# A gated cross-attention block: the attention tile normalised once, and its query brought to both partition halves by two identity matmuls

## What is computed

```
x += tanh(gx[0]) * attention0(layernorm(x), ctx, ctx)      # 32 query heads of 8, 8 key heads; keys = values = ctx
x += tanh(gf[0]) * experts(layernorm(x))                    # 64 experts, top 8 of each row, and a shared one
x += tanh(gx[1]) * (attention1(layernorm(x), ctx, ctx) @ Wc.T + bc)   # 16 query heads of 16, 4 key heads
x += tanh(gf[1]) * fp8_mlp(layernorm(x))                    # 256 -> 1024 -> 256, relu squared, emulated fp8
```

## Time and profile before

| | |
|---|---|
| runs (3), device time | 1719.53 us median, 1709.69 to 1721.87 |
| profiled execution, span | 1714.7 us |
| granted clock of PE, mean over the span | 0.803 of full speed |
| first attention | up to about 296 us |
| experts | about 296 to 1168 us |
| second attention | about 1168 to 1520 us |
| mlp | the rest |

### The profile page before, as it was taken

How to read it: one execution, slowest core, us unless ns; L and a number is a source line. 1 busy time by engine, 2 the same in 40 slices (tenths; PEclk the granted TensorE clock), 3 DMA queues, 4 the chain that set the end, 5 groups by cost and what they waited for, 6 DMA issues and landing times.

```text
span 1714.7 us, 32329 instructions
## 1 busy us (share of the span) xinstructions
PE 1178.8 (69%) x9122; PEld 778.6 (45%) x9132; DVE 1084.7 (63%) x2699; ACT 783.1 (46%) x1599; POOL 883.5 (52%) x846
## 2 busy tenths in 40 slices
PE   4999998133333299999678777871676777846775
PEld 2566665112221266666555555650454444532243
DVE  5899996666666466666444454442765555747898
ACT  3566665122222166666445454441343333433574
POOL 2343343266666633333377777715888888516100
PEclk9999999555555599999777887785788888878878
DMA  9555554032323599999899999984344434100011
GB/s 209 161 151 154 148 154 135 15 115 104 111 106 110 154 281 308 310 301 304 206 242 237 252 246 248 247 199 101 53 54 55 55 55 55 28 1 1 13 37 49
DMA packets 283470, 247.09 MB, mean 144 GB/s; under 512 B 117584, under 2 KB 270032, under 8 KB 282960
## 3 DMA queue, kind: packets, MB, share of 16 engines
q1 hardware_dynamic: 234192, 169.99, 38.9%
q0 software_dynamic: 49152, 75.53, 20.8%
HBM read 111.93 MB, written 117.77 MB: 134 GB/s over the span
## 4 chain that ended last, share of the span: by engine, by line
DMA 24%; DVE 20%; PE 18%; POOL 16%; issue 13%; SPq 4%; ACT 3%; DVEq 1%; POOLq 0%; ACTq 0%
DMA xs<-V 13%; POOL x L632 11%; DMA arena<-xs 8%; PE bank L1493 4%; DVE arena L1318 3%; DMA xs<-arena,V 2%; PE bank L1369 2%; POOL rs L575 2%; PE bank L1381 2%; DVE arena L971 2%; PE bank L1355 2%; PE bank L1569 2%; PE bank L1370 2%; SPq L518 2%; DVE arena L1316 2%
## 5 line engine op out<-in xcount | busy, mean ns | idle before, releaser
L632 POOL DMA_INDIRECT x<-ys,idx x256 | 404.1, 1578 | 129.2 <-issue 57.6
L650 POOL DMA_INDIRECT xs<-V x192 | 187.1, 974 | 207.7 <-DMA xs<-V 188.5
L1493 PE MATMUL bank<-arena,region 128*128 128x128 f16 x2496 | 253.2, 245 | 1.6 <-ACT arena L834 0.9
L834 ACT COPY arena<-bank 128x640 f16<-128x640 f16 x192 | 132.3, 689 | 190.2 <-PE bank L1569 188.2
L1569 PE MATMUL bank<-arena 128*128 128x128 f16 x1440 | 145.2, 240 | 105.3 <-DMA arena<-xs 101.5
L1381 PE MATMUL bank<-arena 128*72 128x256 f32 (+1 forms) x768 | 212.0, 417 | 0.1
L1493 PEld LDWEIGHTS bank<-arena,region 128*128 (+1 forms) x2496 | 187.0, 111 | 19.2 <-issue 6.2
L1569 PEld LDWEIGHTS bank<-arena 128*128 128x128 f16 x1440 | 97.0, 107 | 113.3 <-DMA arena<-xs 85.4
L573 POOL TENSOR_TENSOR ve<-mv,epsilon 128x1 f32<-128x1 f32 x96 | 39.5, 412 | 202.0 <-DVE mv L912 180.0
L1381 PEld LDWEIGHTS bank<-arena 128*72 128x72 f32 (+1 forms) x768 | 117.2, 158 | 46.4 <-issue 13.5
L982 DVE TENSOR_REDUCE arena<-bank 128x8 f32<-128x512 f32 x192 | 124.1, 675 | 15.5 <-PE bank L1355 14.3
(11 more groups left out here) (204 smaller groups left out, 2557.6 us busy)
## 6 DMA issues: line engine op xcount, KB each, us to landing
ys<-arena SPq DMA_DIRECT2D x96, 512.0 KB
arena<-xs SPq DMA_DIRECT2D x288, 160.0 KB
xs<-idx SPq DMA_DIRECT2D x52, 256.0 KB, 2.4
arena<-in_wpairs SPq DMA_DIRECT2D x32, 256.0 KB, 2.6
arena<-in_wpairs SPq DMA_DIRECT2D x128, 64.0 KB, 2.5
x<-ys,idx POOLq DMA_INDIRECT x256, 6.3
out<-arena SPq DMA_DIRECT2D x16, 256.0 KB, 2.2
xs<-idx SPq DMA_DIRECT2D x52, 64.0 KB, 2.1
```

Source lines behind the costliest of these rows:

```text
L632: pool.indirect_dma_start(tile_x(t), None, ys[t // HT], bass.IndirectOffsetOnAxis(ap=idx[:, t, k:k + 1], axis=0), compute_op=ALU.add).then ...
L650: pool.indirect_dma_start(xs[t // HT], bass.IndirectOffsetOnAxis(ap=at_row[:, t, n % 8:n % 8 + 1], axis=0), ROW[t % NROW], None).then_inc( ...
L834: act.copy(XTP[g % 2][q], tpm[n % 2]).then_inc(R_["xt"], 1)
L1493: mm = pe.matmul(o, lhs(a, w, k), rhs(a, w, k), start=(n == 0), stop=(n == 3 * KT - 1))
```

## The change

`norm` writes one destination. XG loses its first copy: a group is now 64 columns and the maxima's. L1435 turns columns 0 to 71 in place of 64 to 135. Where L1422 was one transpose for a group, there are now two plain fp32 matmuls with the identity as the moving operand, the 64 columns of XG as weights, the first into PSUM partitions 0 to 63, the second into 64 to 127. The waits and the semaphores stay as they are.

```diff
--- before.py
+++ after.py
@@ -247,7 +247,7 @@
 
 
     W0 = C + 8
-    XG = [carve([G, C + W0]) for _ in range(2)]
+    XG = [carve([G, W0]) for _ in range(2)]
     KM = carve([2 * 8 * S], F16)
     Q1 = [carve([G, P], F16) for _ in range(2)]
     Q2 = [carve([G, P], F16) for _ in range(2)]
@@ -914,9 +914,7 @@
             def norm(t, j, layer, dst, src):
                 l = LNS[layer]
                 dve.wait_ge(l["rs"], STAT_BASE[layer] + t + 1)
-                for d in dst[:-1]:
-                    dve.tensor_scalar(d, src, mv[:, j, 0:1], rs[:, j, :], ALU.subtract, ALU.mult)
-                dve.tensor_scalar(dst[-1], src, mv[:, j, 0:1], rs[:, j, :], ALU.subtract, ALU.mult).then_inc(l["out"], 1)
+                dve.tensor_scalar(dst, src, mv[:, j, 0:1], rs[:, j, :], ALU.subtract, ALU.mult).then_inc(l["out"], 1)
 
             def biggest(dst, src, done):
                 dve.tensor_reduce(dst, src, AX.X, ALU.max, apply_absolute_value=True).then_inc(done, 1)
@@ -979,7 +977,7 @@
                 def maxima(t, j, u):
                     n = t * nmx + u + 1
                     dve.wait_ge(a["mx_ready"], n)
-                    dve.tensor_reduce(XG[j][:, u * gpu:(u + 1) * gpu, 2 * C:C + w],
+                    dve.tensor_reduce(XG[j][:, u * gpu:(u + 1) * gpu, C:w],
                                       bank[2 + u % 2][:, :].rearrange("p (g k t) -> p g k t", g=gpu, t=S),
                                       AX.X, ALU.max).then_inc(a["mx_done"], 1)
 
@@ -1031,12 +1029,11 @@
 
                         if past(t, 4):
                             dve.wait_ge(F["tp_ready"], t - 3)
-                        norm(t - 2, 2 + j, 3, [XD[j]], tile_x(t - 2))
+                        norm(t - 2, 2 + j, 3, XD[j], tile_x(t - 2))
                     if inside(t + 3):
                         if past(t, -1):
                             dve.wait_ge(a["t2_ready"], t + 2)
-                        norm(t + 3, 1 - j, ln, [XG[1 - j][:, :, r * C:(r + 1) * C].rearrange("p g (k d) -> p g k d", d=d) for r in range(2)],
-                             heads(tile_x(t + 3)))
+                        norm(t + 3, 1 - j, ln, XG[1 - j][:, :, 0:C].rearrange("p g (k d) -> p g k d", d=d), heads(tile_x(t + 3)))
                     if layer == 1 and inside(t - 2):
                         dve.wait_ge(LND["out"], t - 1)
                         dve.tensor_reduce(AM[:, bass.ds(t - 2, 1)], XD[j], AX.X, ALU.max, apply_absolute_value=True).then_inc(F["am_done"], 1)
@@ -1419,8 +1416,8 @@
                         if layer == 1 and past(t, 4):
                             pe.wait_ge(F["xf_ready"], t - 3)
                         for g in range(G):
-                            mm = pe.transpose(bank[0][:, g * P:(g + 1) * P],
-                                              XG[j][:, g, 0:2 * C], ident)
+                            for half in range(2):
+                                mm = pe.matmul(bank[0][half * C:(half + 1) * C, g * P:(g + 1) * P], XG[j][:, g, 0:C], ident, start=True, stop=True)
                         mm.then_inc(a["t1_ready"], 1)
                     if inside(t):
                         values(t, j, 0)
@@ -1432,7 +1429,7 @@
                         if layer == 1 and past(t, 2):
                             pe.wait_ge(a["x_done"], t - 1)
                         for g in range(G):
-                            mm = pe.transpose(bank[1][0:w, g * P:(g + 1) * P], XG[1 - j][:, g, C:C + w], ident)
+                            mm = pe.transpose(bank[1][0:w, g * P:(g + 1) * P], XG[1 - j][:, g, 0:w], ident)
                         mm.then_inc(a["t2_ready"], 1)
                     if inside(t - 1) and layer == 1:
                         pe.wait_ge(a["on_ready"], t)
```

## The result

The changed kernel takes 1718.4 us (median of 20 runs, 1713.6 to 1727.2) and the kernel before 1710.5 (20 runs taken beside them): a ratio of 1.0052, 95% interval 1.0034 to 1.0070. That is 0.5% slower, which is clear over 20 runs; the first three runs of the kernel before alone have a median of 1719.5, above the changed kernel's. One run of the kernel before took 2526.7 us and is left out of the comparison. The profiled execution has a span of 1719.8 us against 1714.7.

A forecast was written before the change was run, and what follows sets the result against it. DVE's loop was taken to bound the first attention and mostly POOL's gathers the second. Terms 6.3 + 2.4 − 0.7 = +8.0 us gave 1727.5 on the 1719.5 median, own range 1722 to 1733, 1715 to 1756 with rivals.

The forecast's parts named there:

- What bounds it: First attention: a loop through DVE sets 8.15 us a tile, PE alone 7.93; second attention: mostly POOL's gathers.
- DVE: One of two norm passes goes per tile and layer, saving 0.40 us, not 1.16; in the first attention it falls into DVE's pause.
- one use: First attention: the removed pass lets the first two L982 finish 0.22 us sooner when PE moves up against L1028.
- PE's term: Query transposes: eight fp32 matmuls take 0.97 us in place of 0.50, +0.47 a tile, range 0.36 to 1.22.
- the rival with long steps: Query matmuls take nine steps of 0.133 us, +0.70 a tile; +16 us in all, 1735 us; chance 0.14.
- the serial rival: fp32 records in different PSUM halves don't overlap, +1.22 us a tile; +33.5 in all, 1753 us; chance 0.23.
- Sum, first attention: Tile goes from 8.15 to 8.40 us: +6.3 over 25 tiles, +2.4 for five earlier ones, nil for the first two.
- they take all: First attention, 32 to 72 us: five early no-wait tiles each bear the full 0.47 us, +2.4 together.
- Second attention: PE's extra time hides under POOL; −1.1 for gathers, +1.2 in the last four tiles, −0.8 in the first two: −0.7 us.
- The −1.1 for POOL's gathers: Second attention: the first gather after a norm, 1.61 us with L919 beside it against 1.56 next, gains 28 x 0.04 us.
- The +1.2 of the four tiles at the end: Second attention's last four tiles: PE waits 0.32 us for L1028, so 0.15 of each +0.47 shows, the first two whole.
- the rival "no effect": TensorE's extra stays under 0.22 us, so the first attention keeps 8.15; only the second's −1.9 remains, 1718 us; chance 0.08.

The follow-up runs named there:

- PE's half alone: Kernel before with the eight new matmuls put in but both norm passes kept: ratio 1.0030 (1.0013 to 1.0046) to the kernel before, period 8.36.
- the two runs with other orders: Changed kernel with its eight matmuls reordered: all four lower-half ones first, ratio 1.0140; lower and upper in groups of two, 1714.1 us beside 1709.6.
- by twos: Changed kernel, matmuls ordered lower half of groups 0 and 1, upper of 0 and 1, then 2 and 3 likewise: 1714.1 us beside 1709.6, single run.

## Why the prediction was right, point by point

**What bounds it.** Right. The 8.15 was DVE's loop, PE's own 7.93 stood behind it (8.15 held with two transposes more, and 7.93 came out with the addition moved), and the norm passes were outside the loop (the first pass left out, 8.15).

**DVE.** Right that the pass lies in the pause, that it isn't worth 1.16, and that the one left keeps 1.16. Its size was 0.32 to 0.33 us and not 0.40: with both, the first L982 starts 1.51 us after the first pass (151.38 − 149.87), with one 1.18 (100.55 − 99.37). Its "one use", to let L982 keep up with PE, wasn't needed: with both passes PE still reaches 8.36, and DVE has 0.57 us to spare (PE's half alone).

**PE's term.** The forecast was +0.47 and the measured one is +0.43: from the second L1355 to the first values matmul 153.90 − 153.09 = 0.81 before, 95.61 − 94.43 = 1.18 after, and the first line of values is 1.95 in place of 1.89 long. The size came out well because two errors met. I had nine steps in strict order; there are eight pairs, 8 x 0.109 = 0.87, my lower bound: 0.10 too much. (At 0.109 a step the rival with long steps, 0.133, is out as well.) And I took the 0.50 as the price of the four transposes alone; their first step of 0.17 in place of 0.11 belongs to the change of form, 0.06 too much on the side that goes. The change of form itself costs nothing net, as forecast: before, 0.10 ahead of L1422 and 0.06 in its first step; after, 0.10 ahead of L1378 and 0.06 in its first step, which is the 1.95 in place of 1.89. So what is added is eight steps for four, 4 x 0.109 = 0.44, and that is why all four transposes made twice gave the same 8.36. That the new records took the forecast 0.97 to the next work is luck too: it was to be nine steps, and it is eight and the 0.10.

The prediction's rule from the Trainium skill (TensorE: Matmul & The Clock Gate, Part 3, The mechanism), that loads overlap matmuls in flight only between different row groups, would have given the serial rival; the loads of both halves begin together here (0.14 us for two), while matmuls run. The same section's strict order of matmul starts would have excluded what the two runs with other orders show.

**Sum, first attention.** The 25 intervals from the seventh query turn to the last take 209.2 us in the changed kernel and 203.6 before, +5.6, for 6.3 forecast. The early ones cost 37.77 − 36.34 = 1.4 without a fall of the clock, for 2.4. From the L1422 at 32.4 to that at 71.9 there are four intervals and not the five that I counted, and "they take all" holds for two of them (+0.43 and +0.44). The other two take 0.27 to 0.28: there PE waits for DVE L982 ahead of L1355, 0.40 us in the kernel before (second profile) and 0.24 in the changed one, and that difference takes up the rest. What comes ahead of the third turn and behind the last moves the end by −0.47. Together that is 5.60 + 1.43 − 0.47 = 6.6, for 8.7.

**Second attention.** +1.0 us (332.5 against 331.5), for −0.7. The −1.1 for POOL's gathers wasn't there: they average 1.584 us in 1235 to 1470 us, and 1.586 before. The first gather behind the norm still takes 1.61 (at 1337.19); no norm pass is beside it any more, but a DVE reduction (L1039) now stands there, so the pass was not the reason for the 1.61, or not the only one. The +1.2 of the four tiles at the end isn't visible either in the last three intervals: 3 x 6.53 = 19.59 us, against 6.17 + 6.67 + 6.69 = 19.53. Which tiles make the +1.0 isn't settled, given its spread. This was the part with the thinnest evidence.

**The total.** +8.0 us, measured +8.9 by the ratio; the two attentions in the profiles, without the early falls of the clock, give 7.6. That the total is this near is partly luck: the first attention was forecast 2.1 us too high and the second 1.7 too low. The median of before was forecast from three runs (1719.5) that were high among its 20 (1710.5), so 1727.5 is 9 us above the measured 1718.4 for that reason and not for the change. It also puts the measured time below the forecast's own 1722 to 1733 and on the 1718 of the rival "no effect"; in microseconds alone the two can't be told apart. What excludes that rival is the period, 8.36 where it needs 8.15, and the ratio. And "most likely reads as no change" underrated the measurement: twenty runs of each gave an interval of 0.34% to 0.70%, where I had reckoned with 1%.

## What to carry to other kernels

A busy share near 100% doesn't say who sets the period: compare where a matmul starts after a wait with where one starts that waited for nothing. The difference is the room, and here it gave the periods of three experiments (two transposes more, four more, the addition moved) to a hundredth of a microsecond. Work taken from an engine outside its critical loop only widens its pause; look for a step inside the loop that can be moved into the pause, which gained 0.3% here while the change lost 0.5%. Where two small matmuls write different PSUM halves, alternate the halves in program order: 8.36 us a tile here, 8.42 by twos, 8.85 with one half first.
